# Staging the second head pair from the split buffers, and the transposes of the outputs at other steps

## The reference

```
x = x + 0.5 * ffn(layernorm(x), gate, gate_up, down)     # 32 experts, 8 per token, capacity 128
x = x + attn(layernorm(x), W_kv_down, ..., W_o)          # 16 heads of 8, causal, 32 shared rotary rows
x = x + 0.5 * ffn(layernorm(x), gate, gate_up, down)

c_kv = x @ W_kv_down;  k = c_kv @ W_k_up;  q = x @ W_q   # split into heads of 8 columns
scores = q k^T + q_rope k_rope^T, / sqrt(40), causal, softmax, @ v, @ W_o
```

## Time and profile before

| | us |
|---|---|
| median of 3 runs | 548.78 |
| lowest, highest | 548.47, 550.87 |
| the profiled execution's own time | 550.67 |
| its span, first to last instruction | 549.0 |
| TensorE busy | 517.1 (94%) |
| VectorE, ScalarE, GpSimd busy | 420.2, 256.3, 98.1 |

### The profile page before, as it was taken

How to read it: one execution, slowest core, us unless ns; L and a number is a source line. 1 busy time by engine, 2 the same in 40 slices (tenths; PEclk the granted TensorE clock), 3 DMA queues, 4 the chain that set the end, 5 groups by cost and what they waited for, 6 DMA issues and landing times.

```text
span 549.0 us, 11100 instructions
## 1 busy us (share of the span) xinstructions
PE 517.1 (94%) x3534; PEld 330.4 (60%) x3559; DVE 420.2 (77%) x1425; ACT 256.3 (47%) x430; POOL 98.1 (18%) x215
## 2 busy tenths in 40 slices
PE   5988999989799899999999999999999987999996
PEld 2856677774356456565565555556544644676775
DVE  5786888885889677778788777878831898798875
ACT  1574222244533456666565666656577641222212
POOL 2120000002593103021221203122131130000000
PEclk8799999999999899999999999999999998999999
DMA  9895300000045001010000101000000180000002
GB/s 181 138 251 199 77 2 2 2 2 3 1 153 184 29 21 41 2 51 9 31 30 22 38 3 53 7 32 29 0 2 1 38 223 2 1 2 2 1 3 77
DMA packets 25095, 26.71 MB, mean 49 GB/s; under 512 B 6704, under 2 KB 18576, under 8 KB 25040
## 3 DMA queue, kind: packets, MB, share of 16 engines
q1 hardware_dynamic: 23024, 23.54, 16.1%
q10 hardware_dynamic: 2016, 2.46, 1.3%
HBM read 17.04 MB, written 8.78 MB: 47 GB/s over the span
## 4 chain that ended last, share of the span: by engine, by line
PE 81%; DVE 8%; DMA 4%; ACT 3%; issue 2%; SPq 1%; ACTq 0%; DVEq 0%
PE ps L1651 14%; PE ps L1740 13%; PE ps L1677 13%; PE ps L1342 11%; PE ps L1430 7%; PE ps L1445 5%; PE ps L1459 3%; PE ps L1647 2%; PE ps L1264 2%; PE ps L1333 2%; PE ps L1706 2%; DVE xn L857 2%; DMA kn_d<-nl 1%; DMA x<-in_L_attn_x 1%; PE ps L1582 1%
## 5 line engine op out<-in xcount | busy, mean ns | idle before, releaser
L767 ACT ACTIVATE probs<-ps 128x1024 f32<-128x1024 f32 (+3 forms) x192 | 146.1, 812 | 96.8 <-PE ps L1677 96.6
L1185 DVE TENSOR_REDUCE mxh<-ps 128x1 f32<-128x512 f32 (+2 forms) x176 | 114.8, 687 | 29.1 <-PE ps L1651 28.5
L1651 PE MATMUL ps<-Kst,Qst 120*128 120x512 f32 (+3 forms) x384 | 129.2, 402 | 3.9 <-DMA Qst<-qn_d 2.6
L1677 PE MATMUL ps<-Qst,Kst 121*128 121x512 f32 (+3 forms) x384 | 94.4, 351 | 0.8 <-ACT probs L767 0.7
L1651 PEld LDWEIGHTS ps<-Kst,Qst 120*128 120x128 f32 x384 | 66.2, 191 | 46.1 <-DVE mxh L1185 17.3
L515 POOL TENSOR_SCALAR_AFFINE_SELECT probs<-probs 128x256 f32<-128x256 f32 x128 | 51.5, 408 | 199.8 <-ACT probs L767 198.5
L1182 DVE CUSTOM_DVE_ANT_0 summed<-ps,maskf 128x384 f32<-128x384 f32 (+1 forms) x128 | 74.3, 618 | 13.5 <-PE ps L1651 13.5
L1740 PE MATMUL ps<-probs,Vst 128*32 128x512 f32 (+3 forms) x768 | 81.8, 499 | 0.1
L1677 PEld LDWEIGHTS ps<-Qst,Kst 121*128 121x128 f32 x384 | 67.2, 191 | 15.1 <-ACT probs L767 5.7
L1342 PE MATMUL ps<-onehot,xp 128*128 128x512 bf16 (+1 forms) x250 | 65.9, 385 | 4.5 <-DVE onehot L936 2.6
L936 DVE TENSOR_SCALAR onehot<-iotab,posm 128x128 bf16<-128x128 bf16 (+1 forms) x352 | 60.4, 250 | 0.2
(11 more groups left out here) (179 smaller groups left out, 622.7 us busy)
## 6 DMA issues: line engine op xcount, KB each, us to landing
wgn<-in_L_ffn_gate_up_proj SPq DMA_DIRECT2D x8, 384.0 KB, 6.4
guT_d<-gus SPq DMA_DIRECT2D x6, 384.0 KB, 5.2
gus<-guT_d SPq DMA_DIRECT2D x6, 384.0 KB, 6.1
Kst<-kn_d SPq DMA_DIRECT2D x28, 64.0 KB
Qst<-qn_d SPq DMA_DIRECT2D x28, 64.0 KB
wdn<-in_L_ffn_down_proj SPq DMA_DIRECT2D x8, 192.0 KB, 7.6
dnT_d<-dns SPq DMA_DIRECT2D x6, 192.0 KB, 5.9
dns<-dnT_d SPq DMA_DIRECT2D x6, 192.0 KB, 7.2
```

The source lines that it names most:

```text
L767: e.activation(probs[n % RING][:, 2 * b:2 * b + 2, lo:BANK], ps[:, 2 * b:2 * b + 2, lo:BANK], ACT.Exp, scale=SCALE).then_inc(probs_ready, 1)
L1185: e.tensor_reduce(to, s.rearrange("p (q k) -> p q k", k=w), AX.X, ALU.max).then_inc(mx_ready, 1)
L1651: ins = e.matmul(ps[:, bank, i * w:(i + 1) * w], Qst[p][h][0:ROWS, column(b, jt * P):column(b, jt * P) + P], Kst[p][h][0:ROWS, column(b, o ...
L1677: ins = e.matmul(ps[:, 2 * b + h, lo:BANK], Kst[p][h][0:ROWS + 1, column(b, kt * P):column(b, kt * P) + P], Qst[p][h][0:ROWS + 1, column(b ...
```

## The change

1. Pair 1's rows no longer come from DRAM. Behind each split SyncE copies the rows of heads 2 and 3 from `nh` and `nl` straight into `Kst[1]` and `Qst[1]`: six DMAs of 8 rows by 512 columns for each u, 48 in all, in place of eight stores and 16 loads. SyncE's shift row for pair 0 (`stage_shift(0, 0, 0)`) stands behind the fifth of the eight groups.
2. All 16 stores to DRAM go to ScalarE's queue; for u = 0 to 4 they stand inside `nope_whole`, ahead of the copy three units later.
3. GpSimd waits, before it writes `nh` again for u = 6 and 7, until all 24 copies of the first half have landed.
4. `turn_out` and `turn_maxima` stand at steps 2, 5 and 8 in place of 1, 3 and 5; in the last pair the one at step 5 stays.
5. In the first front the last `positions` stands ahead of `turn_weights(3)`, with two products of zeros before it; the opening has 18 products of zeros in place of 12; the second front ends with 20 in place of 8.

```diff
-LATETURN, OLDOUT, EARLYTURN, NEWOUT = 0, 1, 3, CLOSES[0] + 2
+LATETURN, OLDOUT, EARLYTURN, NEWOUT = 0, 2, 5, 8
...
+STAGED = 16 * 2 * 3 * NC
...
-            for part in range(2):
-                if part == 0:
-                    for u in range(NC):
-                        store_nope(e, u)
+            def stage_first(u):
+
+                side, c = NOPES[u]
+                to, parts = ((Qst, (nl, nh, nh)), (Kst, (nh, nh, nl)))[side]
+                e.wait_ge(nh_ready, u + 1)
+                e.wait_ge(nl_ready, u + 1)
+                for h in range(2):
+                    for r, src in enumerate(parts):
+                        rows = slice(ROPE3 + r * HD, ROPE3 + (r + 1) * HD)
+                        e.dma_start(raw(to[1][h][rows, piece(c)]), raw(src[u % NB][(2 + h) * HD:(3 + h) * HD, :])).then_inc(stage_in[c % HALFQ][1], 16)
+
+            for u in range(2 * NC):
+                stage_first(u)
+                if u == NC:
                     stage_shift(0, 0, 0)
-                for u in range(part * NC, (part + 1) * NC):
-                    e.wait_ge(nope_stored[u], 32)
-                stage_pair(1, 1, part)
+            for u in range(2 * NC):
+                e.wait_ge(nope_stored[u], 32)
             stage_shift(0, 0, 1)
...
                 if u >= NB:
                     e.wait_ge(nope_stored[u - NB], 32)
+                    e.wait_ge(stage_in[0][1], STAGED)
...
                 if u >= len(nw):
-                    e.wait_ge(nl_ready, u - len(nw) + 1)
+                    store_nope(e, u - len(nw))
...
-                if g < RING:
-                    store_nope(e, NC + 2 * g)
-                    store_nope(e, NC + 2 * g + 1)
+                if g == 0:
+                    store_nope(e, 2 * NC - 3)
+                elif g == 1:
+                    store_nope(e, 2 * NC - 2)
+                    store_nope(e, 2 * NC - 1)
...
-            idle_work(7, 12)
+            idle_work(7, 18)
...
             positions(0, 2)
+            idle_work(1, 2)
+            positions(0, 3)
             turn_weights(3)
-            positions(0, 3)
...
-                    if n == NEWOUT:
+                    if n == (CLOSES[0] + 2 if last else NEWOUT):
...
-            idle_work(0, 8)
+            idle_work(0, 20)
```

More of the change, by code:

```diff
@@ L459, in _ @@
             for part in range(2):
-                e.sem_inc(stage_in[part][0], 128)
+                e.sem_inc(stage_in[part][0], STAGED)
             e.wait_ge(consts_in, 32)
@@ L1638, in maxima @@
                     if m == 0:
-                        e.wait_ge(stage_in[0][p], 128 * (half + 1))
+                        e.wait_ge(stage_in[0][p], 128 * half + STAGED)
                     elif m == EARLYU:
-                        e.wait_ge(stage_in[1][p], 128 * (half + 1))
+                        e.wait_ge(stage_in[1][p], 128 * half + STAGED)
                     bank = ring_bank(unit_place(m))
```

## The result

| | before | changed |
|---|---|---|
| median of 20 runs each, us | 549.13 | 553.26 |
| lowest, highest | 546.14, 552.54 | 550.23, 557.69 |
| profiled execution's own time, span | 550.67, 549.0 | 550.23, 548.5 |
| mean granted clock of the profiled execution | 0.984 | 0.994 |

The ratio is 1.0073, 95% interval 1.0052 to 1.0093: slower, by 2.9 to 5.1 us. The forecast was 544.0, with a range of 542.7 to 546. The execution profiled with the change is the fastest of its 20, the one before lies above its median; the two traces are nearly equally long (549.0 and 548.5) and the medians are not. So the traces are compared stretch by stretch.

The account below looks back on a forecast made before the run. TensorE, busy 94%, was taken to bound the kernel. Terms -2.64 - 1.5 + 0.3 - 0.8 - 0.6 = -5.2 from the 548.78 median gave 543.5; with 0.5 given back, 544.0, range 542.7 to 546.

Parts of the forecast that it names:

- part 1: Staging pair 1 from the split buffers: 48 copies at 0.40 us an issue remove the 2.64 stall and its half clock.
- rival D: Staging: an issue costs 0.735, TensorE's first scores are 7.3 late, second half 2.5 more; 556.0 in all; chance 0.07.
- break-even at 0.43: GpSimd's added wait for the first 24 copies: no delay of V up to an issue every 0.43 us.
- C: Staging: issues take about 0.55, V ends at 175.9, half clock returns; 547.7, no change that can be told; chance 0.11.
- Stall and half clock of the first round: Attention's first round: TensorE's stall on pair 1's loads goes whole, -2.64, and the low clock behind it, -1.5.
- Wait on V: GpSimd's added wait before u = 6: V ends at 172.3, no delay, but +0.3 charged for the small margin.
- The shift row: Pair 0's shift row on SyncE: issued behind 30 copies at 167.0, landed by 170.3, ahead of 173.05.
- Turns: Transposing steps moved in seven pairs: a wait for a bank goes, 0.12 a pair, -0.8; ends -2 and +1.
- `positions`: First front, last positions ahead of turn_weights(3): of 1.85 only the gather's second wait is bought, -0.6; ends 0 and -0.7.
- Zeros in the first front: Six further zero products at the start: TensorE still idles at 10 us, so 0; ends -2 and +0.2.
- rival B: The first front keeps its full clock: the forecast and 2 us more gained, 542.0; chance 0.13.
- Second front: Twelve more zero products: 0.4 lost and clock gained both lie ahead of the one-hot wait, 0; ends +0.4 and -0.1.

## Why the prediction was wrong

**The step that failed** is the price of an issue in part 1: "I take 0.40, between the two loads". Measured: 0.667 from start to start in the even part of the queue, and 0.75 over the 24 copies that GpSimd waits for. It was rival D's condition ("from 0.60 an issue on"), and D's evidence, the shift rows at 0.735 each, was the only SBUF to SBUF row; it was set aside with a chance of 0.07 because its two sides differ in shape. The nearer row was the one with the same two memories, not the one with the same shape. With the break-even at 0.43 beside a value of 0.40, a range of 0.33 to 0.735 should have carried more than 0.18 for C and D together.

Point by point:
- Stall and half clock of the first round, -2.64 - 1.5: right in size (4.08 by the windows, 0.15 of it the turns), by luck. The copies land near 188 and not 177. Before, TensorE asked for them 183.74 - 179.48 = 4.3 after its first weighted sums, which would be 188.3 now: the stall went because TensorE was late as well. Where only GpSimd's wait and the shift row were freed, it came back with 7.28.
- Wait on V, +0.3: measured +6.9, and 1.6 more before the first weighted sums (33.04 - 24.57 = 8.47, less 6.85 of idle time), where the half clock lies. D's own sum, 7.3 late, fits, since 0.75 a copy is what the first half cost; the measured total, 553.26, lies under D's 556.0. D's further 2.5 for the second half did not come: the second half went out at 0.667, and TensorE asked later than D had it, behind the half clock.
- The shift row, "issued at 167.0": measured 173.13. That chain was priced with the same 0.40 and would have held TensorE nearly as long by itself, as the run in which GpSimd waits for its own buffers shows (6.95).
- Turns, -0.8: right. The mean of the five inner rounds is 31.884 before, 31.882 with the staging alone, 31.737 changed: 0.147 a pair, 1.0 for seven.
- `positions`, -0.6: the wait went as described; 0.9 in the traces.
- Zeros in the first front, 0 with "the clock averaged 0.52" as before: open. Of the seven traces above a mean clock of 0.98 with 18 products, five have no half clock in the first front and two have 6.8 us; all six with 12 have 3.4 to 10.2. So in the profiled pair rival B's gain was there, 3.1 at the gather. In the medians it does not show (12 against 18: 542.15 and 543.14), and over the runs the mean granted clock gives nearly as much half clock for the changed kernel as for the one before (13.5 and 13.9 us by 2 x (1 - clock) x span). What part of the difference in medians lies there is not shown.
- Second front, 0: right; the gather starts at 453.76 and its second part waits 1.12 for the one-hot tiles.
- **Outside the span**, a term the prediction did not have. It counted 1.67 around the span. That is so in every run of the kernel before (1.67 to 1.76), but only in the profiled run of the changed one; its 19 others spend 2.3 to 3.0 there, median 2.5. That is +0.8.

The sum with measured terms: +6.9 (V) + 1.6 (the rest of that stretch) - 4.1 (old round) - 0.9 (turns of the six other pairs) - 0.9 (positions) + 0.8 (outside) = +3.4, inside the measured 2.9 to 5.1. The remaining 0.7 to the 4.1 between the medians is below what the runs can resolve.

Neither rule of the Trainium skill named in the prediction was where it failed. "DMA: Bandwidth & Descriptors" (Why a DMA increments its semaphore by 16 and not by 1) led to the load on the DMA engines. By that rule the copies of 16 rows would be spread over 16 engines and not 8, so the run with 32 copies changes that load together with the number of issues and does not separate the two. The landing does: the 24th copy was there 2.1 us after its issue began, against 1.8 for a small copy, so there was no queue on the engines worth several microseconds. "Trainium Kernel Development and Optimization" (Key Constraints) says that several issuing engines save only issue time. No run here divides the copies between two queues, but the trace shows that issue time can be the whole of it: the 48 copies and the shift row hold SyncE from 151.08 to 186.67, 35.6 us, in a stretch where the first half was wanted after 9.5 (GpSimd at 160.59) and, by the times of the kernel before, all after 29 (183.74 - 154.95).

## What to carry to other kernels

Price a burst of small DMAs by issue pitch times count on its queue before looking at bytes, take the pitch from a row with the same pair of memories, and compute the break-even; if it lies inside the range, the slower case deserves a large share. List everything that stands in the same queue or waits for something in it: freeing one chain that ends with two others gains nothing, while cutting the count shortens all. Rows that nobody reads can be made to hold a second copy, so that two copies become one.

## What the runs showed of the hardware

- A copy of 8 rows by 512 columns inside SBUF took 0.625 us of SyncE's time in the changed kernel. In the version with 32 copies one of 16 rows (twice the bytes) took 0.542 and one of 8 rows 0.66 to 0.67 (medians).
- The time of an issue did not follow TensorE's clock (in the execution at 0.82 the copies still took 0.625), and was the same after the last store's issue at 174.83 as in the even part before it.
- Time outside the span was about 2.5 in nearly all unprofiled runs of the six kernels that have both 18 and 20 products of zeros, and 1.7 in those with 12 or 8 in either place, whatever the rest. What is spent there is open.
- The clock fell 4.4 us into a gap of 6.9 on TensorE in the changed kernel, 1.2 us into one of 2.3 with 32 copies, and 1.6 us after one of 2.64 before the change. It did not fall in that round where the longest wait was 0.4.
- Half clock in the first front that ended by about 16 us moved the gather by up to 0.9 us, and where it lasted to 20 us or later by about 3 (20.5 us from the first transpose of `xn` to the gather without it, 23.4 to 23.7 with it).
